# Sampling stage: products laid out with the summed index innermost in PSUM, distances in two 64-row halves, the tensor engine's loop written out

## The reference

```python
# bsz=4, NH=8 heads, NP=8 points, d=16, L=256; Hl=256, Wl=1
off = (query @ soff_w + soff_b).reshape(bsz, L, NH, 1, NP, 2)
aw = softmax((query @ attw_w + attw_b).reshape(bsz, L, NH, NP), axis=-1)
# px, py from off; then for every image, head, query and point
sampled = _bilinear(v, px, py, Hl, Wl)                  # (bsz, NH, L, NP, d)
msda = einsum('bhqpd,bhqp->bqhd', sampled, awt)         # sum over the 8 points
```

## Time and profile before

| | us |
|---|---|
| median of 3 runs (lowest, highest) | 281.02 (280.61, 281.54) |
| the profiled execution | 280.97 |
| its span, first to last instruction | 279.2 |
| PE busy | 228.0 |
| DVE busy | 207.4 |
| ACT busy | 182.2 |
| POOL busy | 48.3 |

### The profile page before, as it was taken

How to read it: one execution, slowest core, us unless ns; L and a number is a source line. 1 busy time by engine, 2 the same in 40 slices (tenths; PEclk the granted TensorE clock), 3 DMA queues, 4 the chain that set the end, 5 groups by cost and what they waited for, 6 DMA issues and landing times.

```text
span 279.2 us, 7567 instructions
## 1 busy us (share of the span) xinstructions
PE 228.0 (82%) x2920; PEld 158.4 (57%) x2920; DVE 207.4 (74%) x474; ACT 182.2 (65%) x273; POOL 48.3 (17%) x64
## 2 busy tenths in 40 slices
PE   0899469999999999859999777988987506899984
PEld 0579327676767776746898765665656403233352
DVE  5766897999999999965416877788858957598412
ACT  8768888989998989047614537767566392465610
POOL 7004919900000000010000200000000577100000
PEclk9999858999999999995999999999999855999999
DMA  5930000000000000492000000000000015493002
GB/s 149 362 122 4 0 0 2 0 2 0 0 0 0 0 0 0 133 388 84 0 2 1 0 2 0 0 2 0 4 0 4 28 58 160 140 441 157 0 2 75
DMA packets 8548, 16.22 MB, mean 58 GB/s; under 512 B 720, under 2 KB 5072, under 8 KB 8272
## 3 DMA queue, kind: packets, MB, share of 16 engines
q1 hardware_dynamic: 8016, 14.90, 14.9%
q0 software_dynamic: 512, 1.05, 1.2%
HBM read 12.80 MB, written 3.15 MB: 57 GB/s over the span
## 4 chain that ended last, share of the span: by engine, by line
PE 44%; issue 43%; ACT 7%; DMA 2%; SPq 1%; DVE 1%; DVEq 0%; ACTq 0%
PE ps L1358 13%; PE ps L1342 9%; PE ps L1661 8%; ACT arena L593 5%; PE ps L1684 2%; DMA r_sb<-in_rows 2%; PE ps L1259 1%; PE ps L1724 1%; PE ps L1644 1%; PE ps L1312 1%; DMA late<-slot_rows 1%; PE ps L1288 1%; PE ps L1300 1%; PE ps L1263 1%; PE ps L1733 1%
## 5 line engine op out<-in xcount | busy, mean ns | idle before, releaser
L593 ACT ACTIVATE arena<-ps,one_less_sq 128x1024 bf16<-128x1024 f32 x64 | 68.7, 1114 | 7.4 <-PE ps L1342 7.2
L1358 PEld LDWEIGHTS ps<-arena 128*128 128x128 bf16 x1536 | 47.6, 96 | 19.7 <-issue 7.6
L1358 PE MATMUL ps<-arena 128*128 (+1 forms) x1536 | 50.4, 184 | 2.1 <-ACT arena L593 2.1
L1342 PE MATMUL ps<-wide,sel 128*128 (+1 forms) x128 | 39.7, 394 | 7.8 <-ACT arena L593 5.9
L983 DVE TENSOR_REDUCE msda<-wide 128x768 f32 x32 | 45.2, 1456 | 0.0
L978 DVE TENSOR_TENSOR wide<-ps,wide 128x768 f32<-128x768 f32 x32 | 29.8, 952 | 4.2 <-PE ps L1358 4.2
L507 POOL DMA_INDIRECT slot_rows<-nrm,slots x16 | 16.1, 1006 | 66.2 <-ACT nrm L726 61.6
L1661 PE MATMUL ps<-arena,w_sb 128*32 x48 | 23.3, 632 | 1.2 <-ACT sel L780 1.2
L1024 DVE TENSOR_REDUCE t_k<-ps 128x2 f32<-128x512 f32 x32 | 20.5, 682 | 0.0
L662 ACT ACTIVATE wide<-ps 128x512 f32<-128x512 f32 x32 | 17.3, 595 | 1.4 <-PE ps L1495 1.3
L1669 PE MATMUL ps<-late,w_sb 128*32 128x512 f32 x80 | 16.5, 663 | 0.0
(11 more groups left out here) (315 smaller groups left out, 504.7 us busy)
## 6 DMA issues: line engine op xcount, KB each, us to landing
arena<-in_w_t SPq DMA_DIRECT2D x1, 4096.0 KB, 15.0
wide<-in_w_t SPq DMA_DIRECT2D x1, 4096.0 KB, 14.7
w_sb<-in_weights SPq DMA_DIRECT2D x1, 1544.0 KB, 9.2
slot_rows<-t_c SPq DMA_DIRECT2D x2, 768.0 KB, 10.7
late<-slot_rows SPq DMA_DIRECT2D x6, 256.0 KB, 3.4
x_sb<-in_x SPq DMA_DIRECT2D x4, 128.0 KB, 2.2
out<-xn SPq DMA_DIRECT2D x2, 256.0 KB, 2.2
r_sb<-in_rows SPq DMA_DIRECT2D x1, 288.0 KB, 4.2
```

What stands on the lines that cost most here:

```text
L593: nc.scalar.activation(hot[:, u, 2 * c:2 * c + 2, :, :], ps[:, 2 * (c % 2):2 * (c % 2) + 2, :].rearrange("r p (b q) -> r p b q", b=B), ACT ...
L1342: ins = nc.tensor.matmul(ps[:, 2 * (c % 2) + p % 2, :], sel[:, bass.ds(i % 4, 1), p, :].rearrange("k h j -> k (h j)"), terms_t[:, bass.ds( ...
L1358: ins = nc.tensor.matmul(ps[:, 4 + b, p * NK * DH:(p + 1) * NK * DH], hot[:, u, p, b, :], rhs, start=(s == 0), stop=(s == PARTS - 1))
```

## The change

Three things are changed. First, a bank of gathered values holds (channel, point, row) instead of (point, row, channel): each gather matmul writes its 48 columns with 24 words from one channel to the next. DVE's product reads and writes in that order with the weight repeated along the outer index, and the reduction runs over neighbouring numbers. Second, the rows of `terms` are ordered (half of the points, head, term, 4 points), so that points 0 to 3 lie in rows 0 to 63 and points 4 to 7 in rows 64 to 127. A distance matmul then uses 64 rows, and a pair is point c and point c + 4, one in each half. `sel` has the same matrix in both halves, 16 in place of 32; `sel_row` and `sel_low` hold their scale and bias. Third, PE's `Fori` over heads becomes a Python loop: all 8 heads are written out, and the addresses that were computed in registers are constants.

```diff
-        sel_low = sb("sel_low", [P, 4, NP])
+        sel_low = sb("sel_low", [P, 4, NP // 2])
+        sel_row = sb("sel_row", [P, 4, NP // 2])
...
+        by_half = terms[:, :, :, :, :].rearrange("q t h c p -> q (t h c p)").rearrange(
+            "q (x a h c p) -> q x a h c p", a=2, h=4, c=4, p=4)
...
-            "q (s b n d) -> q s b n d", s=2, b=2, d=DH)
+            "q (s b d n) -> q s b d n", s=2, b=2, d=DH)
...
             def selectors(which):
                 for n in which:
-                    h, p = n // NP, n % NP
-                    at = 4 * NP * h + p
+                    h, p = n // (NP // 2), n % (NP // 2)
                     ins = nc.scalar.activation(sel[:, h, p, :], minus_2j[:, :], ACT.Identity,
-                                               scale=ident[:, at:at + 1], bias=sel_low[:, h, p:p + 1])
+                                               scale=sel_row[:, h, p:p + 1], bias=sel_low[:, h, p:p + 1])
...
-            selectors(range(0, 12))
+            selectors(range(0, 6))
...
-            selectors(range(12, 3 * NP))
+            selectors(range(6, 12))
...
-            selectors(range(3 * NP, 4 * NP))
+            selectors(range(12, 16))
...
-                    nc.scalar.activation(hot[:, u, 2 * c:2 * c + 2, :, :],
+                    nc.scalar.activation(hot[:, u, c:c + 5:4, :, :],
...
-            nc.vector.tensor_tensor(sel_low[:, :, :], by_term[:, :, 1, :], by_term[:, :, 2, :],
+            nc.vector.tensor_tensor(sel_row[:, :, :], by_term[:, 0, :, 0, :], by_term[:, 1, :, 0, :], ALU.add)
+            link(nc.vector.tensor_tensor(sel_low[:, :, :], by_term[:, 0, :, 1, :], by_term[:, 0, :, 2, :], ALU.add))
+            link(nc.vector.tensor_tensor(sel_low[:, :, :], sel_low[:, :, :], by_term[:, 1, :, 1, :], ALU.add))
+            nc.vector.tensor_tensor(sel_low[:, :, :], sel_low[:, :, :], by_term[:, 1, :, 2, :],
                                     ALU.add).then_inc(sel_low_ready, 1)
...
-            link(nc.vector.tensor_tensor(terms[:, :, :, 1, :], by_head(pair), by_head(pair), ALU.mult))
-            nc.vector.tensor_copy(terms[:, :, :, 0, :], by_head(pair))
+            for a in range(2):
+                ins = nc.vector.tensor_tensor(by_half[:, :, a, :, 1, :], halves_of(pair, a), halves_of(pair, a), ALU.mult)
+            link(ins)
+            for a in range(2):
+                nc.vector.tensor_copy(by_half[:, :, a, :, 0, :], halves_of(pair, a))
             dve.wait_ge(sq_ready, 1)
-            nc.vector.tensor_tensor(terms[:, :, :, 2, :], by_head(pair_sq), terms[:, :, :, 1, :],
-                                    ALU.subtract).then_inc(terms_ready, 1)
+            for a in range(2):
+                nc.vector.tensor_tensor(by_half[:, :, a, :, 2, :], halves_of(pair_sq, a), by_half[:, :, a, :, 1, :],
+                                        ALU.subtract).then_inc(terms_ready, 1)
...
-                        g = ps[:, 4 + 2 * c:6 + 2 * c, 0:NP * NK * DH].rearrange("q b (n d) -> q b n d", d=DH)
+                        g = ps[:, 4 + 2 * c:6 + 2 * c, 0:NP * NK * DH].rearrange("q b (d n) -> q b d n", d=DH)
...
-                                                w.unsqueeze(3).to_broadcast([P, 2, NP * NK, DH]),
+                                                w.unsqueeze(2).to_broadcast([P, 2, DH, NP * NK]),
...
-                                                prod[:, c, :, :, :].rearrange("q b n d -> q b d n"),
-                                                AX_X, ALU.add).then_inc(prod_free, 1)
+                                                prod[:, c, :, :, :], AX_X, ALU.add).then_inc(prod_free, 1)
...
-                for p in (2 * c, 2 * c + 1):
-                    ins = nc.tensor.matmul(ps[:, 2 * (c % 2) + p % 2, :],
-                                           sel[:, bass.ds(i % 4, 1), p, :].rearrange("k h j -> k (h j)"),
-                                           terms_t[:, bass.ds(i // 4, 1), u * HALF:(u + 1) * HALF].rearrange(
-                                               "k g q -> k (g q)"))
+                for a in range(2):
+                    rows = slice(HROWS * a, HROWS * a + HROWS)
+                    ins = nc.tensor.matmul(ps[:, 2 * (c % 2) + a, :], sel[rows, i % 4, c, :],
+                                           terms_t[rows, i // 4, u * HALF:(u + 1) * HALF])
                 ins.then_inc(dist_mm, 1)
...
+                by_point = ps[:, 4 + b, 0:NP * NK * DH].rearrange("q (d p k) -> q p k d", d=DH, p=NP)
                 for p in range(NP):
                     for s in range(PARTS):
-                        rhs = val_p[s][:, b, bass.ds(i, 1), :, :].rearrange("r h k d -> r (h k d)")
-                        ins = nc.tensor.matmul(ps[:, 4 + b, p * NK * DH:(p + 1) * NK * DH], hot[:, u, p, b, :], rhs,
+                        ins = nc.tensor.matmul(by_point[:, p, :, :], hot[:, u, p, b, :], val_p[s][:, b, i, :, :],
                                                start=(s == 0), stop=(s == PARTS - 1))
...
-            with pe.Fori(0, NH - 1) as i:
-                sample(i, False)
-            sample(NH - 1, True)
+            for i in range(NH):
+                sample(i, i == NH - 1)
```

More of the change, by code:

```diff
@@ L838, in _ @@
             dve.wait_ge(ident_ready, 1)
-            by_term = ident[:, :].rearrange("k (h c p) -> k h c p", h=4, c=4)
-            nc.vector.tensor_tensor(sel_low[:, :, :], by_term[:, :, 1, :], by_term[:, :, 2, :],
+            by_term = ident[:, :].rearrange("k (a h c p) -> k a h c p", a=2, h=4, c=4)
+            nc.vector.tensor_tensor(sel_row[:, :, :], by_term[:, 0, :, 0, :], by_term[:, 1, :, 0, :], ALU.add)
+            link(nc.vector.tensor_tensor(sel_low[:, :, :], by_term[:, 0, :, 1, :], by_term[:, 0, :, 2, :], ALU.add))
+            link(nc.vector.tensor_tensor(sel_low[:, :, :], sel_low[:, :, :], by_term[:, 1, :, 1, :], ALU.add))
+            nc.vector.tensor_tensor(sel_low[:, :, :], sel_low[:, :, :], by_term[:, 1, :, 2, :],
                                     ALU.add).then_inc(sel_low_ready, 1)
@@ L911, in _, with halves_of @@
             nc.vector.tensor_scalar(pair[:, :, :], y_half[:, :, :], ROUND, -ROUND, ALU.add, ALU.add).then_inc(pair_ready, 1)
-            def by_head(t):
-                return t[:, :, :].rearrange("q t (h p) -> q t h p", p=NP)
+            def halves_of(t, a):
+                return t[:, :, :].rearrange("q t r -> q (t r)").rearrange("q (x h a p) -> q a x h p", h=4, a=2, p=4)[:, a, :, :, :]
             dve.wait_ge(pair_ready, 1)
-            link(nc.vector.tensor_tensor(terms[:, :, :, 1, :], by_head(pair), by_head(pair), ALU.mult))
-            nc.vector.tensor_copy(terms[:, :, :, 0, :], by_head(pair))
+            for a in range(2):
[3 more added lines that the diff above has]
+                nc.vector.tensor_copy(by_half[:, :, a, :, 0, :], halves_of(pair, a))
             dve.wait_ge(sq_ready, 1)
-            nc.vector.tensor_tensor(terms[:, :, :, 2, :], by_head(pair_sq), terms[:, :, :, 1, :],
-                                    ALU.subtract).then_inc(terms_ready, 1)
+            for a in range(2):
+                nc.vector.tensor_tensor(by_half[:, :, a, :, 2, :], halves_of(pair_sq, a), by_half[:, :, a, :, 1, :],
+                                        ALU.subtract).then_inc(terms_ready, 1)
             dve.wait_ge(proj_ready, 4)
@@ L1318, in _ @@
                 values(b)
-            pe.wait_ge(terms_ready, 1)
+            pe.wait_ge(terms_ready, 2)
             pe.wait_ge(proj_ready, 4)
@@ L1326, in _ @@
                     nc.tensor.transpose(ps[:, g, 64 * n:64 * n + 64].bitcast(BF16),
-                                        terms[:, t, 4 * g:4 * g + 4, :, :].rearrange("q h c p -> q (h c p)"),
+                                        by_half[:, 2 * t + g, :, :, :, :].rearrange("q a h c p -> q (a h c p)"),
                                         ident_b[:, :]).then_inc(terms_mm, 1)
```

## The result

The changed kernel is slower: 297.35 us median (294.91 to 299.61, four runs) against 280.81 (279.71 to 281.54) for the kernel before, ratio 1.057 (95% interval 1.052 to 1.062). The profiled execution took 295.46 us, span 293.7, 14.5 us longer than the one before. It was forecast at 274.9; rival (a), strided results at half rate, gave 294. The sign that was named for a wrong forecast is there: in the loop PE has no gaps, at a round of 5.79 us.

A forecast was written before the change was run, and what follows sets the result against it. ACT and PE were taken to wait for each other, DVE 0.4 us behind; round -4.2, loop start -0.2 and tail -1.7 made -6.1 us against 280.97, giving 274.9. The range was 273 to 295.

The forecast's parts named there:

- rival (a): Gathers in the sampling loop: strided results go out at half rate, 41 ns each, +13, 294 us; chance 0.30.
- The strided result: Gather matmuls writing columns 24 words apart: taken to start every 25 ns still, with 33 and 41 ns kept as cases.
- rival (b): Gathers in the sampling loop: an in-between 33 ns each, step 1.20, round 4.9, +1.8, 283 us; chance 0.08.
- The reduction: DVE's reduction in the sampling loop: about 950 ns over neighbours instead of 1456, 16 us less DVE work.
- rival (c): DVE's reduction keeps its 1.45 us because the stride was not its cost: 277.5 us; chance 0.06.
- The halves: PE's distance pairs: step 1.015 us for 1.03, no PE gain, but a pair complete 0.2 us sooner after its start.
- Rival (d): PE's distance pairs: no changeover cost between bf16 matmuls, ACT's wait 0.1 to 0.2 a round less, 272.5; chance 0.05.
- The written-out loop: PE's loop over heads: 0.75 us of PE a head goes; fetching code taken as nothing, bound +10.
- Rival (e): PE's written-out loop: PE starves on fetched code, 1 us a packet, +4 net, 285 us; chance 0.03.
- The period of 4.43 us: The sampling loop's round: four ACT one-hots of 1.03 plus a 0.31 wait, for 4.71 before; -4.2 us over fifteen rounds.
- The tail: After the last gather: DVE's faster end lets PE's transposes start sooner, 117.9 for 119.6, a gain of 1.7 us.
- Ahead of the loop: Work before the loop: sixteen fewer selectors give nothing, DVE's terms cost 0 to 0.5 us, taken as 0.

The follow-up runs named there:

- experiment 1: The kernel before with the strided layout alone, with product and reduction following it; loop, distances and selectors unchanged: 301.21 us, ratio 1.074.
- experiment 2: The changed kernel with gathers, product and reduction of the kernel before: 277.03 us, ratio 0.989.
- experiment 6: The kernel before with one edit: DVE's product reads PSUM with a step of 16 words, the reduction runs over neighbours: 280.45 us, ratio 0.9988.
- experiment 10: The kernel of experiment 3 with PE's order changed: two distance pairs at a round's start, none before its last gathers: 273.57 us, ratio 0.975.
- experiment 3: The changed kernel, but gathers write 48 neighbouring columns and DVE's product reads PSUM with a step of 16 words: 273.72 us, ratio 0.977.
- experiment 5: The kernel of experiment 4 with every bank's data one word later, so pairs lie across 8-byte lines: 299.42 us, ratio 1.068.
- experiment 7: The kernel of experiment 6 with PE's loop over heads written out, distances still over 128 rows: 277.72 us, ratio 0.987.
- experiment 9: The kernel of experiment 3 run again unchanged, beside experiment 10: 272.56 us, ratio 0.971.
- experiment 4: The changed kernel with two channels side by side, so gathers write aligned runs of two words: 274.33 us, ratio 0.978.
- experiment 11: The kernel of experiment 4 with four channels side by side, so gathers write runs of four words: 285.54 us, ratio 1.016.
- experiment 8: The kernel of experiment 3 with PE's distances running five steps ahead of the gathers instead of four: 274.56 us, ratio 0.981.

## Why the prediction was wrong

The step that failed is "The strided result", with its choice "I take 25 ns and keep both others as cases". It measured 42.5 ns, the upper bound and a little. I went by "of PE writing PSUM the nearest row is the gather itself", but that row held no stride: it could bound the cost from below and could not choose. The two rows that did bear on it, 5 ns of room above 20 and DVE's price for a stride, both pointed up. Experiments 1 and 2 put all of the loss on this one step, and the changed kernel's 80 ns at half clock show it to be clocks of PE, two a column. That leaves nothing for rival (b), 33 ns.

The other steps, one by one:

- What bounds the kernel (ACT and PE wait for each other, a faster DVE alone gains little): shown by experiment 6, a round of 4.714 us with DVE 1.9 us a head lighter. The 1.03 us for ACT's pace was an upper value: experiment 10 has 1.00.
- The reduction: 950 ns forecast, 942 measured. That a stride was its cost, rival (c), is settled.
- The halves: two matmuls 3 ns apart, the pair 0.115 us after the last gather and the gathers 0.318 after the pair, in experiment 3; forecast 0.11 and 0.32. The changed kernel and experiment 5 have 0.152 for the first; why it grows with the slower gathers is not shown. Rival (d) falls.
- The written-out loop: a head is 0.47 us shorter in experiment 7 than in 6, and fetching costs nothing that shows, though more packets of instructions came (23 in the changed kernel, 13 before): in experiments 3 and 7 rounds 3 to 15 agree within 4 ns. Rival (e) falls.
- The period of 4.43 us, for a kernel with gathers at 25 ns: experiment 3 has 4.36. Start to start ACT waits 0.25 us for the forecast 0.31 (idle: 0.17). One latency was too long: the gathers start 0.055 us after the fourth one-hot's end, where I had 0.15; the others were right within 0.01.
- The tail, -1.7: -1.8 in the changed kernel and in experiment 6.
- Ahead of the loop: the first gather started 0.9 us sooner, 39.48 for 40.36; I had taken 0.2. But the kernel of experiment 3, with the same work ahead of the loop, started it at 40.40, so the 0.9 can't be put down to the change. The selectors gave nothing, as forecast.
- The forecast as a whole, 274.9, is the time of a kernel with all three edits and no stride: experiment 3 has 273.7 and, in experiment 9, 272.6; experiment 4 has 274.3. In the trace of experiment 3 the first to the last gather take 4.8 us less than before and the tail 1.8, for the forecast 4.2 and 1.7, so the terms are right too and not only their sum.
- A slip in rival (b): four steps of 1.20 us are 4.80, not 4.9, which makes its case 281.3 us and not 283.

Rival (a) had the mechanism and undersized two terms: 42.5 ns for 41, and the changeover 0.152 for 0.13. Its step was 1.40 for a measured 1.45, its round 5.60 for 5.79: 15 x 0.19 = 2.9 us too little. Its +13.0, with these 2.9, 0.2 for the last round and -1.8 for a start and an end that were sooner than forecast, is +14.3; +14.5 was measured. That (a)'s 294 came so near has luck in it: two errors of 3.1 and -1.8 us partly cancel. The range, up to 295, ended at this rival's centre, with no room for its own error, and both the profiled execution (295.46) and the median (297.35) lie beyond it.

## What to carry to other kernels

Before PE is made to write a layout that suits its reader, count how many successive output columns share an aligned 8-byte line of PSUM: here aligned pairs were free and single columns cost two clocks each, which took a matmul of 48 fp32 columns from 25 to 42.5 ns. The reader of PSUM may be able to turn the data for nothing: DVE's product read with a step of 16 words at full speed. Where three engines hold each other in a ring, relieving the third alone gives the loop nothing (experiment 6), but with the other two relieved it is worth having (4.466 us a round in experiment 2, 4.359 in 3). And a rival that hangs on an unshown cost must lend the range its own error too, not only its centre.

## What the runs showed of the hardware that was not expected

**A later stage takes back what an earlier one gains.** After the turning of `msda` the program is the same in experiments 3 and 10. The third took 158.9 us for it, the tenth 160.5. Busy time by stretch (length, PE, PEld, DVE, ACT, POOL, granted clock), first experiment 10:

```profile
146.00:156.40 10.40, 6.87 (x57) 6.16 (x56) 8.44 (x21) 5.56 (x10) 1.40 (x3) 1.00 0.00 0
156.40:166.60 10.20, 9.67 (x47) 7.60 (x45) 6.63 (x10) 5.41 (x8) 0.00 (x0) 0.50 0.01 2
```

and experiment 3, the same work 2 us later:

```profile
148.00:158.40 10.40, 6.88 (x57) 6.16 (x57) 8.75 (x23) 5.56 (x10) 1.91 (x3) 1.00 0.01 2
158.40:168.60 10.20, 8.50 (x78) 6.23 (x77) 7.44 (x12) 6.67 (x11) 0.00 (x0) 1.00 0.00 0
```

In the first row of each PE did the same, 57 matmuls in 6.9 us of 10.4. Then in one kernel the granted clock fell to 1.2 GHz for 10.2 us and PE started 47 matmuls instead of 78; in the other it stayed at 2.4 GHz. The kernel of experiment 6 has such a stretch from 162 us on and took 161.5 us after the turning, where the kernel before, at full clock there, took 159.6. The traces of experiments 1 to 8 and 11 divide the same way. The part after the turning took 160.1 us in experiment 1, 160.2 in 7 and 163.3 in 11, and each has some 10 us at half clock that begin 42 to 45 us after the turning, as in 6 and 10; it took 158.3 to 159.6 us in the kernel before, the changed kernel and experiments 2, 3, 4, 5 and 8, which have none there. So some 1.5 to 2 us, in experiment 11 more, hang on whether this stretch is at half clock, and that is as much as several of the edits above are worth. What decides it stays open: in experiments 3 and 10 PE had done the same just before, in 11 it had been busy 9.3 us of 10.2, and no run here was made to find out.

**A step of 16 bytes costs DVE's reduction more than one of 64**: 1533 ns (experiment 11) for 1440 (experiment 2), and 942 with 4 or 8 bytes. No run here shows a reason.
